# Two-layer graph network with attention on one core: the self products of layer one computed early and kept in DRAM, and new orders for the keys and the attention

## The reference

```python
h = max(layernorm(x), 0)
e_h = rel_embed[rel_id]
for W_r, W_sl, W_el in two_layers:
    self_msg = where(in_degree == 0, h @ W_el, h @ W_sl)
    agg = segment_sum((e_h + h[src]) @ W_r, dst)
    h = rrelu(agg * in_degree**-0.5 + self_msg)
x = x + h
h = max(layernorm(x), 0)
qk, v = h @ Wqk + bqk, h @ Wv + bv
scores = clip(sum(qk[dst] * qk[src], -1) / sqrt(128), -5, 5)
attn = softmax over the edges of each dst
out = segment_sum(attn * v[src], dst) @ Wo + bo
x = x + gamma * norm(out + h) + beta
```

## Time and profile before

| | |
|---|---|
| median of 3 runs | 794.05 us (791.5 to 797.88) |
| the profiled execution, its own time | 796.59 us |
| its span, first to last instruction | 794.8 us |
| granted TensorE clock, mean | 0.924 |
| PE busy | 721.5 us (91%) |
| DVE busy | 515.8 us (65%) |
| ACT busy | 429.9 us (54%) |
| POOL busy | 239.2 us (30%) |

### The profile page before, as it was taken

How to read it: one execution, slowest core, us unless ns; L and a number is a source line. 1 busy time by engine, 2 the same in 40 slices (tenths; PEclk the granted TensorE clock), 3 DMA queues, 4 the chain that set the end, 5 groups by cost and what they waited for, 6 DMA issues and landing times.

```text
span 794.8 us, 15460 instructions
## 1 busy us (share of the span) xinstructions
PE 721.5 (91%) x5799; PEld 537.4 (68%) x5799; DVE 515.8 (65%) x932; ACT 429.9 (54%) x1085; POOL 239.2 (30%) x272
## 2 busy tenths in 40 slices
PE   3566699989899999999999999899999999999995
PEld 2545588879789999888998999444444444444465
DVE  5798999968679777742334333444665757566667
ACT  0557556746566666662112221477676767677671
POOL 6300000000000222200000000266675767666663
PEclk7555579989999999999999999999999999999997
DMA  4102000032310000011232111210000000000000
GB/s 131 46 8 60 17 1 9 7 105 75 95 52 9 8 9 7 10 64 52 72 98 70 39 33 38 96 37 1 1 19 8 13 14 13 13 14 13 4 23 20
DMA packets 39763, 27.89 MB, mean 35 GB/s; under 512 B 5311, under 2 KB 38163, under 8 KB 39686
## 3 DMA queue, kind: packets, MB, share of 16 engines
q1 hardware_dynamic: 38514, 25.89, 11.2%
q10 hardware_dynamic: 1172, 0.98, 0.4%
HBM read 13.28 MB, written 10.80 MB: 30 GB/s over the span
## 4 chain that ended last, share of the span: by engine, by line
PE 73%; DVE 8%; issue 7%; ACT 6%; DMA 2%; SPq 2%; ACTq 1%; POOL 0%; POOLq 0%; DVEq 0%
PE sums L1503 16%; PE sums L1486 15%; PE sums L1091 12%; PE sums L1018 12%; PE sums L1057 8%; DVE work L847 2%; ACT counts L1278 2%; SPq L557 2%; DVE work L841 2%; DMA counts<-in_x 1%; PE sums L1114 1%; PE sums L1025 1%; PE sums L1098 1%; ACTq L1248 1%; PE sums L1032 1%
## 5 line engine op out<-in xcount | busy, mean ns | idle before, releaser
L1582 POOL TENSOR_TENSOR counts<-counts,work 125x500 f32<-125x500 f32 x150 | 165.3, 1102 | 95.6 <-DVE work L1643 88.5
L1057 PE MATMUL sums<-work 125*128 125x196 f16 (+15 forms) x1220 | 156.5, 255 | 19.9 <-DVE work L847 19.8
L1643 DVE SCALAR_TENSOR_TENSOR work<-sums,counts 125x500 f32<-125x500 f32 x150 | 101.7, 678 | 105.5 <-ACT sums L1600 105.5
L1503 PE MATMUL sums<-work 125*128 125x500 f32 (+1 forms) x350 | 159.0, 544 | 7.5 <-DVE work L1643 3.0
L1486 PE MATMUL sums<-work 128*125 128x500 f32 x300 | 150.5, 583 | 0.0
L1595 ACT ACTIVATE sums<-sums,work 125x500 f32<-125x500 f32 (+1 forms) x157 | 102.0, 650 | 75.3 <-PE sums L1486 72.0
L841 DVE TENSOR_TENSOR work<-work,counts 125x3024 f16<-125x3024 f16 (+1 forms) x60 | 114.2, 1904 | 40.5 <-PE sums L1059 36.9
L1059 PE MATMUL sums<-work 125*128 125x10 f16 (+15 forms) x800 | 132.9, 195 | 0.0
L1278 ACT CAST counts<-sums 128x364 f32 (+38 forms) x305 | 131.4, 472 | 2.2 <-issue 0.6
L847 DVE TENSOR_TENSOR work<-work,counts 125x4200 f16<-125x4200 f16 (+15 forms) x120 | 125.4, 1084 | 0.0
L1018 PE MATMUL sums<-counts 125*128 125x250 f16 (+1 forms) x975 | 121.7, 269 | 4.0 <-ACT work L1208 3.8
(11 more groups left out here) (177 smaller groups left out, 685.6 us busy)
## 6 DMA issues: line engine op xcount, KB each, us to landing
first_columns<-counts SPq DMA_DIRECT2D x5, 610.4 KB
counts<-first_columns SPq DMA_DIRECT2D x5, 610.4 KB
counts<-counts SPq DMA_DIRECT2D x5, 468.8 KB
counts<-in_x SPq DMA_DIRECT2D x5, 312.5 KB
h_nodes<-counts SPq DMA_DIRECT2D x5, 312.5 KB
work<-in_x SPq DMA_DIRECT2D x12, 125.0 KB
x_after_messages<-work SPq DMA_DIRECT2D x12, 125.0 KB
h_attention<-work SPq DMA_DIRECT2D x12, 125.0 KB
```

Source lines behind the costliest of these rows:

```text
L1057: pe.matmul(win[:, 0:c, cols], lo[:, k * 2 * LO:k * 2 * LO + 128], m[:, k, h0 * w:(h0 + c) * w].rearrange("p (h d) -> p h d", d=w), start= ...
L1503: last = pe.matmul(ps_o[c % 2][:, 0:cols(u) // n], h3[:, source(c, j + i), :], pbuf[u % PB][:, i * NP:i * NP + cols(u) // n], start=j + i ...
L1582: pool.tensor_tensor(a, a, p, ALU.add).then_inc(acc_done, 1)
L1643: dve.scalar_tensor_tensor(pbuf[u % PB], ps_s[u % 4][0:NP, 0:WIDE], float(np.exp(-CLIP)), counts[0:NP, source(c, j), target(c) * WIDE:(tar ...
```

## The change

It has six parts.

- **Self products early.** `own` loses its transposes and `self` goes. Two new kinds of step take their place at groups 44 to 76: `turn` of chunk c at group 44 + 5c//2 (the same transposes, into PSUM bank 1 or 5; ACT copies them to SBUF) and two groups later `weigh` (the same product with the weights, bank 3 or 7; ACT copies the 125x512 result to SBUF). SP stores each to a new DRAM tensor (`self_layer_one`) and loads chunk 0 back into `t2` and `t1`; chunk c+1 is loaded as soon as the result of chunk c has been stored and has landed. For chunks 3 and 4 ACT issues the load, two groups after the store of the chunk before. At `rest` ACT scales `t2` and `t1` in place.
- **Scaling and splitting of x earlier.** Two scaling activations per group from group 16 on in place of one; `ROUNDS` from (22 to 42) and (30 to 50) to (20 to 30) and (32 to 41); `RESTS` from batches 7 to 14 to 8 to 12.
- **Keys.** The order is 0, 2, 1, 3 on DVE and PE, ACT makes all four first copies and one dummy copy at the very start, the `room` table is made later, `statistics` runs after batch 2.
- **End of layer two.** The sums of the last chunk are cut at blocks 4 and 18, and `h_attention` is loaded in pieces as they finish, the first ahead of the store of x; four scores and two units are begun ahead in place of three and one.
- **Attention.** `last_turn` and `last_qk` stand after units 3 and 5 in place of 1 and 3; `before` runs in the same target chunk in place of the next one, `ending` of the last full chunk is spread later, and POOL does two of its operations.
- The self weights of layer two are loaded at group 180.

```diff
@@ plan
-        slots[s1].append(("self", c, 0))
+    for c in reversed(range(CHUNKS)):
+        g = SELF_AT + c * SELF_STEP // 2
+        slots[g].insert(0, ("turn", c, 0))
+        slots[g + 2].insert(0, ("weigh", c, 0))
@@ ScalarE, layer1
-                    act.copy(htc[:, 0:w], ps1[:, LB * NP:LB * NP + w]).then_inc(ht_out, 1)
+                if kind == "turn":
+                    act.wait_ge(self_pe, turned(c))
+                    act.copy(turns[c % 2][:, 0:w], psum[:, SELF_BANKS[c % 2][0], 0:w]).then_inc(self_act, 1)
+                if kind == "rest":
+                    act.wait_ge(self_in, 16 * (ODD + (c + 1 if c <= DIRECT else CHUNKS)))
@@ ScalarE, the groups
             act_stores = {at_slot["agg", c] + 2: c for c in (2, 3)}
+            act_loads = {at_slot["agg", c] + 4: c + 1 for c in (2, 3)}
+                if g in act_loads:
+                    c = act_loads[g]
+                    act.wait_ge(h1_out, 16 * c)
+                    act.dma_start(P["both"], self_rows(c)).then_inc(self_in, 16)
-                if SCALED <= g < SCALED + NB:
-                    j = g - SCALED
+                for j in range(2 * (g - SCALED), min(2 * (g - SCALED) + 2, NB)):
@@ SyncE, layer two
+                if i == LAST - 1:
+                    sp.wait_ge(L["summed"], CHUNKS)
+                    h3_load(0)
                 sp.wait_ge(L["x2_ready"], i + 1)
@@ attention, TensorE
-            if u == 1:
+            if u == 3:
                 last_turn()
-            if u == 3:
+            if u == 5:
                 last_qk()
@@ attention, VectorE, last chunk
-    LAST_ENDING = ((), (), ((0, 0), (0, 1)), ((0, 2), (1, 0), (1, 1)), ((1, 2), (0, 3)), ((0, 4), (0, 5), (1, 3)), ((1, 4), (1, 5)))
+    LAST_ENDING = ((), (), ((0, 0),), ((0, 1),), ((0, 2),), ((1, 0),), ((1, 1), (1, 2), (0, 3), (0, 4), (0, 5), (1, 3)))
```

360 lines of the change are left out of this document (227 added, 133 removed).

## The result

The changed kernel takes 797.4 us (median of 20 runs, 791.5 to 799.5) where the kernel before, run beside it, takes 794.4 (20 runs). The ratio is 1.0036, with an interval from 1.0019 to 1.0054: slower by a third of a per cent, where 0.8% faster was forecast. The time lies inside the range given, the sign is wrong. The profiled execution has a span of 794.9 us, against 794.8 before, so the two profiles can be laid side by side.

The account below looks back on a forecast made before the run. DVE was taken to bound 58 to 160 us, PE the later counting and the attention. Terms -6.3 + 5 + 0.5 - 12 + 12 - 2.7 - 3 = -6.5 us gave a median of 787.5 us, range 773 to 802.

Parts of the forecast that it names:

- the start: Before the first batches: new key order, early table load and earlier statistics remove DVE's waits, 6.3 us gained.
- groups 16 to 28: Doubled scalings and earlier roundings load ScalarE, so DVE must wait: 5 us lost, from 1 to 7.
- groups 44 to 76: ScalarE's added copies make it and DVE nearly equal, earlier clock helps: 0.5 us lost, from -1.7 to +6.
- PE from there to layer two: PE after 160 us: 42 self products and 57 transposes fewer, 12 us gained.
- waits for loads and stores in it: ScalarE waits for stores to land at groups 122 and 135: 6 us each, 12 lost, from 0 to 25.
- layer two and into the attention: Turn into the attention: h loaded in pieces, first weighted product earlier, 2.7 us gained, from 1 to 4.5.
- the end: Last full chunk's DVE work moved after the last unit or to POOL: 3 us gained, from 1 to 5.
- would show it wrong: Signs: no idle at groups 122 and 135; DVE batches later after the last relation split; ScalarE waiting at any `rest`.
- Rival 1: Stores land in time and ScalarE's loads hold up nothing: 775.5 us, chance 0.20.
- rival 3: PE's stages become bound by DVE, so PE's 12 us less work yields 4: 795.5 us, chance 0.05.
- Rival 2: Early part fully bound by ScalarE, groups 16 to 28 losing 7 and 44 to 76 losing 6: 795 us, chance 0.15.
- rival 4: Slower than before: both waits for ScalarE's loads last 11 us: 801.5 us, 809 with rival 2's early part; chance 0.15.

Follow-up runs that it names:

- e_scale: Changed kernel with one scaling per group again and the old groups for roundings and rests; 791.7 us, ratio 0.9958 to the kernel before.
- e_both: Changed kernel with the edits of e_last and e_scale together; 784.6 us, ratio 0.9854 to the kernel before.
- b_noself: Kernel before with all of the change except the move of turn and self products, plus the edits of e_last and e_scale; 784.4 us, ratio 0.9884, on another chip.
- e_store: Changed kernel with the self-product stores shrunk to 8 columns of 512, loads of the same size reading stored h; 791.0 us, ratio 0.9957 to the kernel before.
- e_actsh: Changed kernel with ScalarE's copies of turned rows and self products cut to 16 columns from the third chunk on; 792.6 us, ratio 0.9969 to the kernel before.
- e_two: Changed kernel with the edits of e_store and e_actsh together; 786.7 us, ratio 0.9935 to the kernel before, on another chip.
- e_keep: Changed kernel with self products of chunks 0 to 5 kept on the chip where x lay, without their stores and loads; 786.5 us, ratio 0.9880.
- e_best6s: Changed kernel with the edits of e_last, e_scale and e_keep, and self products set further apart (SELF_STEP 6, not 5); 773.6 us, ratio 0.9759, on another chip.
- e_last: Changed kernel with the last chunk's x rows in free columns of the counts' planes, without DVE's wait for their store; 789.7 us, ratio 0.9928.

## Why the prediction was wrong

The sum of the prediction beside what the profiles give for the same stretches (us):

| term | forecast | measured |
|---|---|---|
| the start | -6.3 | -6.2 |
| groups 16 to 28, read at batch 13 | +5 | +5.3 |
| groups 44 to 76, read at batch 28 | +0.5 | +7.9 |
| PE from there to layer two | -12 | -14.4 |
| waits for loads and stores in it | +12 | +5.5 |
| layer two and into the attention | -2.7 | +5.6 (-0.8 and +6.4) |
| the end | -3 | -3.7 |
| sum | -6.5 | 0.0 |

The medians differ by +3.0 us where this pair of profiles differs by 0.0; to which term the 3 us belong, no profile here shows.

**The start, the scalings and the end** came as worked out in size. Batch 3 stands 6.2 us earlier in every kernel with the new key order and loads of four. The scalings' loss came later than said, for batch 8 starts at 58.7 us and not near 62, and the rest is lost by batch 11. And it isn't added to the next term as the sum has it: taken back, it leaves 2.8 us at batch 28 and not 5.3 (e_scale). Taken by themselves the scalings cost 2.8 us there and the move 10.3 (e_both against b_noself), the same 13 us divided otherwise, and then the miss in the next term is larger.

**Groups 44 to 76: the step that failed, mis-sized by 7.4 us, beyond its own range** of -1.7 to +6. It held DVE's time and ScalarE's time each against the 38 us of the stretch, found ScalarE at 41, and called the stretch nearly even. Three things were wrong. It took the eight register loads at 0.91 us and put the transfers' effect into one short sentence ("can lengthen the loads"); they took 2.1 us, and the stores, with this, cost 4.1 of the 7.9 us (e_store). The trace before had the price. Beside SP's stores of x, from 58 to 82 us, its loads took:

```profile
L1248 ACTq TENSOR_LOAD <-work x6: 908/1838/2692, 58.2 to 81.7; - x6
```

The prediction read 1.51 us for such a load out of the earlier trace rows; that is the time for which ScalarE stood idle behind it, and the load itself, at 58.2 us, took 2.63. The prediction also counted the added copies as ScalarE's alone, but every carry copy stands behind them, and PE behind the carry copy: 2.5 us by themselves, 1.0 once the transfers are gone (e_actsh, e_two). And it used PE's busy time at the low clock and the hope of a better one as room, where PE in fact gets 1.2 us a chunk more (0.88 and 0.33, its own prices from the earlier trace rows) in front of the product that ScalarE waits for; the 2.7 us that are left are put down to it, without a run that shows it. The copies' own prices were right (0.38 and 0.59 us a pair, 0.97 against 1.05), and the clock came up 22 us earlier, as said.

**PE's saving** was real: 14.4 us in e_keep, 14.3 in e_best6s between batch 28 and layer two, where 12 were forecast. The mark lies at 150 us and the forecast counted from 160: the four self products of chunk 1, at 151 us, and six transposes at 155 are 1.2 us of the difference. DVE had the room.

**The loads from ScalarE** were priced at 12 us and cost 5.5 together with the wait that was priced at nothing. The mechanism was right at group 122: landing 6.9 us (8 estimated), ScalarE idle 3.84 (4.6), PE 2.54 (3.3). Wrong were the second of them, which had no wait at group 135, and the size of the clock's fall: the low level held for 3.4 us behind the gap, which costs 1.7 us at most, where 2.7 were taken. As the fall of 6.9 us at 165 us is gone, the clock from 160 to 200 us is 0.96 and not lower than before; up to 347 us both kernels have about 10 us of the low level. The things that "would show it wrong" all happened in part: no idle time at 135, though there is at 122; DVE's batches later than before from batch 17 on; and ScalarE waits 2.59 us at the `rest` of chunk 5. The allowance of six groups and 10 us counted from the moment at which the load could be issued; SP had first to get its 21 us of other transfers and the store of chunk 4 out, and to wait for that store. Rival 1, the loads holding up nothing, was nearer than the forecast in this term.

**Into the attention: the second step that failed**, 6.4 us lost where 2.7 were to be won. The diff adds one wait to DVE, at the fourth unit, for the store of x's last rows. The prediction goes through loads, scores and waits unit by unit and doesn't name this one. Its two lines are those that the edit of e_last takes out. It accounts for the miss in this term: without it (e_last) product 7 starts 3.2 us earlier than before, 1.7 us of them beyond what layer two brought. That is inside the 1 to 4.5 given. What was needed stood in the rows: a transfer in this stretch is late by microseconds, and the first product of a unit is 1.7 us behind the last.

**Scaling from the chip's memory.** The prediction took 0.50 us for an activation from SBUF against 0.37 from PSUM, and 6.5 us for 50 of them, hidden. The new ones took less (ns least/median/most, the two lines of the scaling):

```profile
L1317 ACT ACTIVATE work<-work,small x25: 386/402/425, 137.0 to 359.8; 125x128 f32<-125x128 f32 x25
...
L1318 ACT ACTIVATE work<-work,small x25: 385/387/410, 137.3 to 360.1; 125x128 f32<-125x128 f32 x25
```

That is 0.034 us more than the 0.368 from PSUM in the one line and 0.013 more than the 0.374 in the other (L1221 before), 1.2 us for 50. Here the estimate from the Trainium skill, VectorE: DVE Perf Modes, section on the errata, 2.2 us for 50, was nearer than the one from the row: the row was of an activation with other operands, two per-partition tables and a source among the counts.

**The rivals.** By the number alone rival 3 (795.5) is nearest, but by luck: PE's stages were not bound by DVE, the saving came in full. Rival 2 (795: the early part bound by ScalarE) is nearest in its account: its sum for the early part (7 and 6 against 5.3 and 7.9) was right, though the stores and not ScalarE alone made half of the second, and it took all the rest from the forecast. Rival 1's premise held for one of the two stores, rival 4's for none: neither wait came near 11 us. None of the rivals had the attention, so the sign could only come right by luck.

What stays open: whose the last 2.7 us of groups 44 to 76 are, and why the store of chunk 3 lands within 3.5 us when that of chunk 2 takes 6.9. The first went out while SP wrote the first columns (DMA share 0.34 at 106 GB/s from 186 to 193 us), the other behind the small moves of keys (0.40 at 68 GB/s from 210 to 214 us): the bytes moved differ the right way, the share does not, and no run tells them apart.

## What to carry to other kernels

Work that is moved to where an engine is idle brings its transfers and its place in the order along: price it by the handshake it stands in front of, and ask first whether it can stay on the chip, since here the move brought nothing that the runs can tell until half of its results were kept there. Read a diff once for its waits alone, above all those for a transfer whose buffer is reused, and give each a landing time from the busiest stretch nearby, not from a quiet one. Here a gain in front of an engine that bounds the stretch stayed nearly whole (of 6.2 us 5.6 through the counting without the move), and in the stretch with the move, where three engines wait for one another in turn, half of 5.3 us was left.

## What was not expected of the hardware

A register load on ScalarE from the chip's own memory costs 0.21 us a value; beside stores of 250 KB its four values take 2.1 us in place of 0.9 (changed kernel against e_store), beside stores of 312 KB up to 2.69 (kernel before), and twenty took 10.86 us once. A store of 62.5 KB took 9.2 us to land behind loads of h at 126 GB/s, one of 125 KB 6.9 us beside 106 GB/s, and a second one of 125 KB at most 3.5 us beside 68 GB/s.

The clock column and the pace of the instructions can disagree: from 58 to 85 us the changed kernel's column says 1.00, but its weight loads take 150 ns, as in the kernel before where the column says 0.50. From 86 us on they take 104. That column is filled up from a record that begins at 85.1 us in this trace and at 5.2 us in that of the kernel before, so a level is checked against the length of one repeated instruction. And less work can be slower: PE's products cut from 256 to 16 columns kept the low level for 30 us longer, and the kernel got no faster for it: batch 28 was 2.3 us later.
